# Regrouped loads, small zeroing pieces, shorter last feed-forwards, and layer B's attention heads turned by a DMA transpose

## The reference, cut to what matters

```
x = x + tanh(g_xattn[0]) * attention_A(ctx, layernorm(x))   # 8 heads of 64, keys = 375 context + 112 latents
x = x + tanh(g_ffn[0])   * experts(layernorm(x))            # top 2 of 8 experts, 256 -> 512 -> 256
x = x + tanh(g_xattn[1]) * attention_B(ctx, layernorm(x))   # 16 heads of 64
x = x + tanh(g_ffn[1])   * bitlinear_ffn(x)                 # quantised 256 -> 1024, depthwise conv of 3 taps,
                                                            # silu, quantised 1024 -> 256
out = softmax(q @ k.T, masked) @ v, per head; then out.reshape(112, heads * 64) @ Wout
```

## Time and profile before

| | us |
|---|---|
| median of 3 runs | 1540.71 (1537.53 to 1558.93) |
| the profiled execution, its own time | 1539.86 |
| its span, first to last instruction | 1538.1 |
| mean granted clock of TensorE | 0.937 of full |
| busy: PE / POOL / DVE / ACT | 1278.3 / 1107.9 / 1053.8 / 979.1 |

### The profile page before, as it was taken

The page is one execution under the profiler, slowest core; times in us unless marked ns, Lnnn a source line. Parts: engine busy times, 40 slices in busy tenths (PEclk is TensorE's granted clock), DMA queues, the critical chain, the costliest instruction groups (busy, mean ns, idle before and its releaser), DMA issues.

```text
span 1538.1 us, 45142 instructions
## 1 busy us (share of the span) xinstructions
PE 1278.3 (83%) x16918; PEld 994.2 (65%) x16918; DVE 1053.8 (69%) x2830; ACT 979.1 (64%) x2319; POOL 1107.9 (72%) x1359
## 2 busy tenths in 40 slices
PE   0778787679878989878999999899999999998852
PEld 0556565557667866656887887667676676766642
DVE  4768788977556656665666666777777777877634
ACT  2778787456455666554656566678777777777631
POOL 4768788687557755466777776788878888787653
PEclk9989999879999989989999999999999999999965
DMA  9599997486999954368999997344555444555310
GB/s 314 134 193 235 246 239 174 83 221 188 218 233 252 233 95 97 73 159 171 247 258 231 269 247 181 79 97 98 105 91 94 90 105 94 106 82 91 79 32 6
DMA packets 438329, 239.96 MB, mean 156 GB/s; under 512 B 388848, under 2 KB 420320, under 8 KB 429024
## 3 DMA queue, kind: packets, MB, share of 16 engines
q1 hardware_dynamic: 408216, 178.51, 55.7%
q10 hardware_dynamic: 26824, 51.22, 10.6%
q0 software_dynamic: 3072, 7.34, 1.6%
HBM read 107.78 MB, written 35.50 MB: 93 GB/s over the span
## 4 chain that ended last, share of the span: by engine, by line
PE 39%; ACT 13%; DVE 12%; POOL 11%; issue 9%; DMA 9%; DVEq 3%; SPq 2%; ACTq 1%; POOLq 0%
PE bank_ring L1088 9%; PE bank_ring L1126 6%; PE bank_ring L1074 5%; PE bank_out L1107 5%; DVE scores L1340 4%; DMA expert_up<-experts_up 4%; ACT scores L849 4%; PE bank_x L1187 3%; POOL probs L654 3%; PE bank_scores L1048 3%; ACT probs L856 3%; PE bank_x L1140 3%; DMA probs_turned<-probs 3%; ACT values L876 2%; DMA context<-in_ctx 2%
## 5 line engine op out<-in xcount | busy, mean ns | idle before, releaser
L654 POOL TENSOR_TENSOR probs<-scores,probs 112x487 f16<-112x487 f32 x384 | 425.0, 1123 | 234.2 <-ACT probs L856 229.1
L849 ACT ACTIVATE scores<-scores,score_min 112x487 f32<-112x487 f32 x384 | 265.8, 693 | 121.0 <-DVE score_min L1340 118.2
L1357 DVE SCALAR_TENSOR_TENSOR values<-bank_ring,values 128x512 f16<-128x512 f32 x192 | 132.4, 689 | 216.4 <-ACT values L876 216.3
L1340 DVE CUSTOM_DVE_ANT_0 scores<-bank_scores,mask 112x487 f32<-112x487 f32 x384 | 238.1, 657 | 2.9 <-PE bank_scores L1048 2.9
L856 ACT ACTIVATE probs<-scores 112x487 f16<-112x487 f32 x384 | 214.2, 604 | 24.4 <-DMA probs_turned<-probs 9.0
L1088 PE MATMUL bank_ring<-weights,kv_B 128*128 128x128 f16 x3072 | 198.3, 223 | 1.2 <-DVE keys L1352 1.2
L876 ACT ACTIVATE values<-bank_ring 128x512 f16<-128x512 f32 x192 | 112.9, 588 | 128.9 <-PE bank_out L1107 125.2
L1088 PEld LDWEIGHTS bank_ring<-weights,kv_B 128*128 128x128 f16 x3072 | 187.2, 100 | 10.5 <-DVE keys L1352 2.0
L1107 PE MATMUL bank_out<-values,probs_turned 128*128 128x64 f16 x4608 | 171.9, 195 | 17.7 <-issue 11.4
L1074 PE MATMUL bank_ring<-kv_B,weights 128*128 128x488 f16 x768 | 181.0, 372 | 0.0
L1107 PEld LDWEIGHTS bank_out<-values,probs_turned 128*128 128x128 f16 x4608 | 160.1, 100 | 21.4 <-issue 14.0
(11 more groups left out here) (230 smaller groups left out, 2470.9 us busy)
## 6 DMA issues: line engine op xcount, KB each, us to landing
expert_up<-experts_up SPq DMA_DIRECT2D x43, 1024.0 KB, 5.5
expert_down<-experts_down SPq DMA_DIRECT2D x43, 512.0 KB, 6.6
raw_weights<-in_weights ACTq DMA_DIRECT2D x8, 1536.0 KB, 10.7
experts_up<-expert_up ACTq DMA_DIRECT2D x8, 1024.0 KB, 4.4
raw_weights<-in_weights ACTq DMA_DIRECT2D x6, 1024.0 KB, 8.0
probs_turned<-probs SPq DMA_TRANSPOSE x384
context_turned_B<-kv_B ACTq DMA_DIRECT2D x16, 375.0 KB, 8.7
kv_B<-context_turned_B ACTq DMA_DIRECT2D x16, 375.0 KB, 3.7
```

What stands on the lines that cost most here:

```text
L654: pool.tensor_tensor(PR[:, u % 4, 1, 0:KEYS], S[:, u % 4, 0:KEYS], PR[:, u % 4, 0, 0:KEYS], ALU.subtract).then_inc(probs_split, 1)
L849: act_e.activation(S[:, u % 4, 0:KEYS], S[:, u % 4, 0:KEYS], ACT.Exp, bias=rmin[:, u % 4:u % 4 + 1], scale=-1.0, accum_out=rsum[:, g % 2, ...
L1340: dve.tensor_tensor_reduce(out=S[:, u % 4, 0:KEYS], in0=bS[u % 2][0:TOK, 0:KEYS], in1=mask[:, m, 0:KEYS], scale=1.0, scalar=3.0e38, op0=AL ...
L1357: dve.scalar_tensor_tensor(vN[:, j % 2, 1].rearrange("p t d -> p (t d)"), bank("v", j)[:], 1 / WSCALE, vN[:, j % 2, 0].rearrange("p t d -> ...
```

## The change

1. **Zeroing.** Nine pieces of at most 5 tiles (640 KB) in place of five of up to 10, one a step, in steps 1 to 9 on SP, ahead of that step's two turns of probabilities.
2. **Start.** ACT's first weight loads wait for context 0. The mask load moves behind context 1 and x 1. x 2 to 5 come in one DMA, x 6 to 15 at step -2.
3. **Layer B's weights** come as 16 DMAs of 256 KB, one a step from step 35.
4. **split_context of the second half** of a context (kb = 1) stands right behind the first half on POOL, before the step's probabilities rather than between its two.
5. **m_gate** goes from early to late in the same step (not for sequences 5 and 15).
6. **Heads of layer B** (groups 16 to 47): ACT rounds `wide` to fp16 in step 4g + 6, DVE subtracts in step 4g + 7, SP turns both halves with one DMA transpose in step 4g + 8, o_proj is in step 4g + 9 instead of 4g + 8. The o_turn task of these groups, ACT's and DVE's reading of its bank are gone.
7. **Last feed-forwards.** New step tables for sequences 13 to 15; the second half of the convolution of 14 (before: of 15 alone) goes from POOL to DVE; f_down of 14 is in step 197, ahead of the feed-forward of 15.

```diff
-ZERO_DMAS = sum(-(-t // XR_SLOTS) for t in TILES)
+ZERO_SLOTS = XR_SLOTS // 2
+ZERO_PIECES = [(b, t, min(ZERO_SLOTS, TILES[b] - t)) for b in range(2) for t in range(0, TILES[b], ZERO_SLOTS)]
...
+F_MIDDLE = {"stats": 13, "rstd": 14, "rows": 14, "round": 14, "turn": 15, "up0": 16, "up1": 17, "sides0": 18,
+            "sides1": 19, "tanh0": 18, "tanh1": 19, "act0": 19, "act1": 20, "max0": 19, "max1": 20, "rate": 21,
+            "scale0": 22, "scale1": 23, "down": 23, "store": 25}
+F_QUICK = {"stats": 14, "rstd": 14, "rows": 14, "round": 14, "turn": 14, "up0": 15, "up1": 15, "sides0": 16,
+           "sides1": 16, "tanh0": 16, "tanh1": 17, "act0": 17, "act1": 17, "max0": 17, "max1": 18, "rate": 18,
+           "scale0": 19, "scale1": 19, "down": 21, "store": 22}
+def on_vector(n, half):
+    return n >= NSEQ - 2 and half == 1
...
 def early(j):
-        if j == 4 * n + 10 + slack(n):
+        if not slack(n) and j == 4 * n + 10:
             tasks.append(("m_gate", n))
...
-        if j == 4 * g + 6 + slack(g):
+        if g < NSEQ and j == 4 * g + 6 + slack(g):
             tasks.append(("o_turn", g))
-        if j == 4 * g + 7 + slack(g):
+        if j == 4 * g + (7 + slack(g) if g < NSEQ else 9):
             tasks.append(("o_proj", g))
...
 def late(j):
+        if slack(n) and j == 4 * n + 11:
+            tasks.append(("m_gate", n))
...
+        wh = kv[0][0:TOK, 0, 0]
...
 SP, start
-            sp.dma_start(mask8[:], mask_in[0]...)                      # before context 1
-            sp.dma_start(X[:, 2:NSEQ], x_in[2:NSEQ]...)
-            sp.wait_ge(zeros_set, 1)
-            for b in range(2): ... five DMAs into xs[b] ...
+            sp.dma_start(mask8[:], mask_in[0]...)                      # after context 1 and x 1
+            sp.dma_start(X[:, 2:6], x_in[2:6]...)
 SP, steps
+            def turn_heads(g):
+                sp.wait_ge(x1_filled, X1_AT[("o_proj", g - 1)])
+                sp.wait_ge(o_split, g - NSEQ + 1)
+                sp.dma_start_transpose(oT[:].rearrange("p a m t -> p (a m) t"), wh[:].rearrange("p a c -> p (a c)"))\
+                    .then_inc(o_turned, 16)
             for j in STEPS:
+                for g in range(NSEQ, PAIRS // 4):
+                    if j == 4 * g + 8:
+                        turn_heads(g)
+                if j == -2:
+                    sp.dma_start(X[:, 6:NSEQ], ...)
+                if 0 <= j - 1 < len(ZERO_PIECES):
+                    zero_rows(*ZERO_PIECES[j - 1])
...
 POOL, steps
                     split_context((j + 4) // 4, 0, 0)
+                    split_context((j + 4) // 4, 1, 0)
...
                 if is_pair(j):
                     split_probs(2 * j)
-                if (j + 4) % 4 == 0 and 0 < (j + 4) // 4 < NSEQ:
-                    split_context((j + 4) // 4, 1, 0)
                 if is_pair(j):
                     split_probs(2 * j + 1)
...
 ACT
+            act_e.wait_ge(ctx_loaded[0], 16)
             load_raw(0, 0, 4, weights_in, 0)
...
-                    load_raw(12 + i, i, 4, weights_in, L1_AT + 4 * i)
+                    at = L1_AT + c
+                    act_e.dma_start(raw4(c), weights_in[:, at * CHUNK:(at + 1) * CHUNK]).then_inc(l1_loaded[c % 8], 16)
...
+            def round_heads(g):                                        # after the step's probabilities
+                act_e.wait_ge(out_normed, g + 1)
+                if g > NSEQ:
+                    act_e.wait_ge(o_turned, 16 * (g - NSEQ))
+                act_e.activation(wh[:, 0], wide[:], ACT.Copy).then_inc(o_hi, 1)
...
 PE
                 elif name == "o_proj":
+                    if n >= NSEQ:
+                        pe.wait_ge(o_turned, 16 * (n - NSEQ + 1))
...
 DVE
+            def split_heads(g):                                        # before split_q of its step
+                dve.wait_ge(o_hi, g + 1)
+                dve.tensor_tensor(wh[:, 1], wide[:], wh[:, 0], ALU.subtract).then_inc(o_split, 1)
```

More of the change, by code:

```diff
@@ L127 @@
            "scale0": 23, "scale1": 24, "down": 26, "store": 27}
[L128 to L134, removed]
+F_MIDDLE = {"stats": 13, "rstd": 14, "rows": 14, "round": 14, "turn": 15, "up0": 16, "up1": 17, "sides0": 18,
[4 more added lines that the diff above has]
+           "scale0": 19, "scale1": 19, "down": 21, "store": 22}
+EARLY_UP, EARLY_MAX, EARLY_RATE, LATE_DOWN = ((NSEQ - 2, 0),), ((NSEQ - 2, 1),), (NSEQ - 3,), (NSEQ - 3,)
+def on_vector(n, half):
+    return n >= NSEQ - 2 and half == 1
 def f_step(n, name):
@@ L152, in early @@
     for g in range(PAIRS // 4):
-        if j == 4 * g + 6 + slack(g):
+        if g < NSEQ and j == 4 * g + 6 + slack(g):
             tasks.append(("o_turn", g))
-        if j == 4 * g + 7 + slack(g):
+        if j == 4 * g + (7 + slack(g) if g < NSEQ else 9):
             tasks.append(("o_proj", g))
     for n in range(NSEQ):
-        if j == f_step(n, "down"):
+        if n not in LATE_DOWN and j == f_step(n, "down"):
             tasks.append(("f_down", n))
-        if n == NSEQ - 3 and j == f_step(n, "rate"):
+        for i in range(2):
+            if (n, i) in EARLY_UP and j == f_step(n, f"up{i}"):
+                tasks.append(("f_up", n, i))
+            if (n, i) in EARLY_MAX and j == f_step(n, f"max{i}"):
+                tasks.append(("f_max", n, i))
+        if n in EARLY_RATE and j == f_step(n, "rate"):
             tasks.append(("f_rate", n))
@@ L183, in late @@
         for i in range(2):
-            if j == f_step(n, f"up{i}"):
+            if (n, i) not in EARLY_UP and j == f_step(n, f"up{i}"):
                 tasks.append(("f_up", n, i))
         for i in range(2):
-            if j == f_step(n, f"max{i}"):
+            if (n, i) not in EARLY_MAX and j == f_step(n, f"max{i}"):
                 tasks.append(("f_max", n, i))
-        if n != NSEQ - 3 and j == f_step(n, "rate"):
+        if n in LATE_DOWN and j == f_step(n, "down"):
+            tasks.append(("f_down", n))
+        if n not in EARLY_RATE and j == f_step(n, "rate"):
             tasks.append(("f_rate", n))
@@ L382, in build @@
         l1_hi, l1_split = sem("l1_hi"), sem("l1_split")
+        l1_loaded = [sem(f"l1_loaded_{i}") for i in range(8)]
         ex_stored = [sem("ex_stored_0"), sem("ex_stored_1")]
@@ L994, in _ @@
                     round_probs(2 * j + 1)
+                for t in early(j):
+                    if t[0] == "f_up":
+                        part(t)
+                for g in range(NSEQ, PAIRS // 4):
+                    if j == 4 * g + 6:
+                        round_heads(g)
                 load_weights(j)
```

81 lines of the change are left out of this document (44 added, 37 removed).

## The result

The changed kernel took 1604.4 us (median of 4 runs, 1595.0 to 1607.7) against 1539.1 for the kernel before on the same chips: a ratio of 1.039, interval 1.030 to 1.047. It is slower by 3.9%, some 60 us by the ratio and 65 by the medians, where 1511 was forecast. Its profiled execution has a span of 1605.0 us.

What follows compares the result with a forecast made beforehand. No one engine bounds the whole: the edits fall into six places, each with its own bound. Their terms, -8 - 2 - 6 - 2 - 3 - 8 = -29, against 1539.9 gave 1511 us, range 1482 to 1543.

Steps and rivals of the forecast that it cites:

- the heads of layer B: Plain layer B, 12 sequences: PE is relieved but doesn't set the pace alone; -3 us in all, from -25 to +12.
- Rival (b): Layer B: the ACT to DVE loop is lengthened, o_proj delays proj_v; slower than before, 1546 us; chance 0.14.
- Rival (a): Layer B: PE is the pace, giving -27 us instead of -3, 1487 us in all; chance 0.18.
- Second batch of tiles: Layer B's second expert batch, four sequences: PE gains 5 us, full DMAs get 11 more; -2, from -6 to +8.
- the PE gain of 5 us: Second expert batch: PE no longer does o_turn, 0.60 us each, two a sequence, four sequences: 5 us gained.
- DVE's subtraction: Heads of layer B: with both operands in SBUF it takes 0.61 to 1.10 us, median 0.75.
- Start and zeroing: Program start: without the zeroing DVE's wait for context 2 goes, -15; pieces in steps 1 to 9 cost +7; sum -8.
- Layer A: Layer A: POOL's earlier mask gains, m_gate's late place costs; -2 us together, from -20 to +15.
- POOL's part: Layer A: split_context moved, the mask comes 1.6 us earlier, counted for 11 waits of PE: -17 us.
- The gate's 1.5 us: Layer A: proj_q waits for late m_gate's drain, some 1.5 us a time; +15 to +17 over 14 sequences.
- Layer B's weights: First expert batch: smaller loads shorten PE's waits for up weights; -6 us, from -20 to +5.
- The end: After the last heads: o_proj some 3 us earlier, f_down out 2.4, halves side by side 2.5; -8, -3 to -12.

Runs made afterwards that it cites:

- first experiment: The changed kernel with the heads of layer B turned by TensorE again and o_proj back in step 4g + 8 (part 6 undone): 1552.9 us, ratio 1.0035.
- sixth experiment: The changed kernel with heads turned by TensorE as before, but o_proj kept one step later, in step 4g + 9: 1579.0 us, ratio 1.021.
- Experiments 2 and 4: The changed kernel with the DMA turn issued one step sooner: 1586.9 us; with o_proj of even groups alone one step later: 1586.1 us.
- fifth: The changed kernel with the DMA turn issued in step 4g + 7 and o_proj back in step 4g + 8: 1557.5 us, ratio 1.0065.
- ninth: The changed kernel with DMA turn in step 4g + 7, o_proj in 4g + 8, m_gate early, zeroing in steps 25 to 27: 1551.7 us, ratio 1.004.
- seventh: The first experiment plus DMA turns of the same shape in layer B on which nobody waits: 1558.9 us, ratio 1.0067.
- tenth experiment: The first experiment with m_gate early again, zeroing pieces still in steps 1 to 9: 1537.7 us, ratio 0.995.
- eighth: The first experiment with m_gate early again and the zeroing pieces in steps 25 to 27: 1534.8 us, ratio 0.990.
- twelfth: The eighth with layer B's weights loaded by four DMAs of four chunks again (part 3 undone): 1550.4 us, ratio 1.0004.

## Why the prediction was wrong

- **The step that failed: the heads of layer B,** "I take -3 in all, from -25 to +12". It measured +46 us in steps 104 to 184, and part 6 as a whole costs about 54 us (first experiment). Two things were wrong in it. First, o_proj's place. The waits of the earlier trace rows were counted as gains at 3.4 us a sequence and cut down for ACT's round; the new waits behind f_turn and f_max were named, but taken for equal. Moved from a step of 6.5 us (ACT's work sets it) to one of 4.95 us (nothing spare) the same task with the same kind of wait costs 1.6 to 3.5 us a time. The sixth experiment shows this alone: 3.8 us in the median sequence, 29 us in steps 104 to 184, 26 us by the times.
- **Second, when the turn arrives.** It was priced as DMA time (1.32 us) and, at the end, as 4.1 us of latency; in layer B its arrival had no price, and no reason was given. At the place shown above the turn is issued only behind two turns of probabilities that wait for POOL, 5 us after its source is ready, and lands after 6.8 us where it meets the reload. Experiments 2 and 4 take away 2.8 us a sequence, which is this half.
- **Rival (b)** named the loop (o_proj delays proj_v, so ACT's values, so the next mask) and gave 1546; it had the mechanism for the first half and the size of half of it. It was also to be fed by the convolution's steps, and those (2 and 3) changed by +0.5 and -0.4 us.
- **Rival (a)** falls as it was priced: with 0.6 us less on TensorE a group (fifth and ninth) a sequence is no shorter. Whether TensorE could shorten steps 1 and 5, where it shows no idle time, no run tests.
- **Second batch of tiles:** -2, from -6 to +8; measured +14. Steps 72 to 104 take 293.9 us with TensorE's turns (first), 300.0 with idle DMA turns besides (seventh), 304.1 with DMA turns at good places (fifth) and 307.1 in the changed kernel. So some 6 us are traffic, some 4 come with the turns being waited for, and some 3 with their places, each from one profile. The terms that failed are the PE gain of 5 us, of which nothing shows, and the wait for the turn, which had no price. The 6 us of traffic lie between the 4 us by the Trainium skill's sentence (page Advanced Engine Details and Errata, section X-Bar Transpose (TRN2)) and the 11 us by the earlier trace rows. In DMA time the seventh experiment has 1.36 us a turn, as the earlier trace rows, and not the half microsecond of that sentence.
- **DVE's subtraction:** 0.68 to 1.68 us, median 1.10, against 0.61 to 1.10 expected. The Trainium skill's rule on two SBUF inputs (page SBUF — State Buffer, section Who interferes with whom) fits: at 1274.0 us a POOL instruction on SBUF starts 0.02 us ahead and lasts 1.14, and the subtraction, 0.68 at its shortest, takes 1.67. In the fifth experiment the subtraction is no shorter (median 1.26 us) and a sequence takes 47.3 us against 47.1, so it costs next to nothing on this path.
- **Start and zeroing:** -15 and +7; measured -9.8 to step 0 and +7.3 in steps 0 to 12. The sum of -8 was -2.5. POOL's mask came at 30.3 instead of the 28 to 29 expected, and PE's first projection not at the mask but 3 us behind it. The step that failed is "POOL's mask at 32.7 is late next": next was POOL's split of a context behind the mask, then DVE's copy (L1640) and PE's turn (L1204), which stands ahead of the projection in PE's order. The +7 of the pieces was about right.
- **Layer A:** POOL's part was about right by the waits (17.7 us went, -17 in the sum), though a few of them hang on the gate's late place. The gate's 1.5 us was right (1.9 measured), and it costs 13 us as a whole against 15 to 17 estimated. Together they were taken as -2; measured were +14 in steps 12 to 72. The tenth experiment shows the gate's 13. A term that the prediction has nowhere is the wait for turned probabilities, in 50 to 300 us, 15.2 us on PE, where the kernel before had 3.5 in 60 to 300. With the zeroing pieces in steps 25 to 27 it is 14 to 22 us (eighth, ninth, twelfth), so their place does not explain it, and its cause stays open. So does how much of the +14 is scatter between executions: steps 12 to 36 took 185 us before, 193 in the changed kernel and 186 to 205 in the experiments, in no order that an edit explains.
- **Layer B's weights:** -6. The wait for up weights fell by 10 us in the changed kernel, but its steps 36 to 56 are 1.6 us longer than before; over all profiles the gain is some 5 us, within the scatter.
- **The end:** -8; measured -5.5. From the mask of step 191 the last norm_out comes 2.8 us sooner (some 5 expected), from there to o_proj it is 8.3 us against 8.4 (2 longer expected), and from o_proj to the last addition 2.6 us less (4.9 expected). So o_proj is 3.0 us earlier, as forecast by two terms that were both too large, and the step that failed is the rest, f_down out of the chain and both last halves side by side. With TensorE's turns o_proj follows norm_out after 7.3 us (first).

## What to carry to other kernels

A task's wait has a price only where its engine has nothing spare, so before moving a task look at how long each step is by place and what sets it; here a wait of 1.4 us in a long step was free, and one of 1.2 to 2.0 us in a short step cost 1.6 to 3.5 us. When work goes to a DMA, go through the issuing queue's order for what stands ahead of it and through the other queues for what is in flight at that moment: here a turn whose median landing is 3.9 us was used 12 us after its source was ready, 5 of them in the queue and 6.8 in landing. And price a new transfer where the DMAs are full, not on the mean.

## What was not expected of the hardware

A DMA transpose of 112 x 1024 fp16 within SBUF took 1.36 us of all 16 DMA engines and landed in 2.9 to 6.8 us. Eight of them added some 6 us in steps 72 to 104, where the DMA share was 0.8 to 1.0, and nothing in plain layer B, where their share was about 0.5. In the kernel before, one context load behind five zeroing transfers of up to 1.25 MB was 21.5 us on its way. Nine of up to 640 KB cost some 8 to 11 us in sum, in steps 1 to 9 and in steps 25 to 27 alike. A DVE subtraction with both inputs in SBUF took 0.68 us beside no POOL instruction and 1.67 beside one that had started just ahead of it.
